# One fused kernel of two graph layers and two expert layers: the last expert layer's rows are placed in groups of chunks 0+1, 2 and 3 instead of 0, 1+2 and 3

## The reference

```
x = x + gnn0(layernorm(x), adj)              # filtered adjacency times features
x = x + ffn0(layernorm(x))                   # 8 experts, top 2, all rows through all experts
x = x + gnn1(layernorm(x), adj)              # normalised adjacency times features, ELU
def ffn1(x):                                 # x here is layernorm(x)
    h = rmsnorm(x, ln1)
    q, k, v = rope(h wq), rope(h wk), h wv                # 4 query heads, 2 key heads of 32
    y = softmax(q k / sqrt(32), causal) v                 # 2048 x 2048 scores
    x = x + y wo
    f = rmsnorm(x, ln2)
    p = softmax(f router_w); tp, ti = top_k(p, 2); tp = tp / (sum(tp) + 1e-9)
    return x + sum over the 2 chosen experts of tp * (silu(f w1) * (f w3)) w2
x = x + ffn1(layernorm(x))
```

## Time and profile before

| what | us |
| --- | --- |
| three runs: lowest, median, highest | 610.11, 612.19, 612.92 |
| the profiled execution, its span | 610.4 |
| PE, DVE, ACT, POOL busy in it | 501.5, 429.3, 314.3, 254.2 |
| attention chunk 2 (12 steps) | about 377.7 to 424.5 |
| attention chunk 3 (16 steps) | about 424.5 to 489.4 |
| chain of chunk 3, first experts' blocks, late row scatters | 489.4 to 531 |
| the other blocks and the way out | 531 to 610.4 |

### The profile page before, as it was taken

The page is one execution under the profiler, slowest core; times in us unless marked ns, Lnnn a source line. Parts: engine busy times, 40 slices in busy tenths (PEclk is TensorE's granted clock), DMA queues, the critical chain, the costliest instruction groups (busy, mean ns, idle before and its releaser), DMA issues.

```text
span 610.4 us, 11302 instructions
## 1 busy us (share of the span) xinstructions
PE 501.5 (82%) x3819; PEld 281.4 (46%) x3819; DVE 429.3 (70%) x1065; ACT 314.3 (51%) x522; POOL 254.2 (42%) x275
## 2 busy tenths in 40 slices
PE   2999986699999799996776888998969657498880
PEld 1533334477777445443322432333412157397770
DVE  6898838888999925757786896999752038166564
ACT  0787985869999001201254453764745334166661
POOL 3000005133436401102364895997353632555562
PEclk9999995999999799999578789999989859599996
DMA  8999954100139250110233522003035447389925
GB/s 302 409 421 422 405 189 149 42 19 20 34 129 411 85 109 0 39 26 15 68 110 99 157 72 60 2 1 104 35 129 177 176 121 222 112 277 384 324 89 175
DMA packets 39570, 93.43 MB, mean 153 GB/s; under 512 B 7488, under 2 KB 24944, under 8 KB 35168
## 3 DMA queue, kind: packets, MB, share of 16 engines
q1 hardware_dynamic: 35072, 86.96, 40.6%
q0 software_dynamic: 2272, 4.69, 2.2%
q10 hardware_dynamic: 2176, 1.13, 0.6%
HBM read 69.39 MB, written 21.00 MB: 148 GB/s over the span
## 4 chain that ended last, share of the span: by engine, by line
PE 54%; DVE 21%; ACT 7%; issue 6%; another core or an unknown queue 5%; DMA 4%; POOL 1%; SPq 1%; DVEq 0%; POOLq 0%; ACTq 0%
PE ps L1578 8%; DVE A L2385 7%; PE ps L1755 6%; PE ps L1489 6%; PE ps L1506 6%; PE ps L1404 5%; PE ps L1859 3%; PE ps L1656 3%; PE ps L1747 3%; DMA R<-in_adj_in 3%; PE ps L1842 2%; PE ps L1603 2%; PE ps L1381 1%; DVE bst L1916 1%
## 5 line engine op out<-in xcount | busy, mean ns | idle before, releaser
L2385 DVE TENSOR_REDUCE A<-ps 128x1 f32<-128x512 f32 (+3 forms) x160 | 86.3, 601 | 13.7 <-PE ps L1656 13.0
L1302 ACT ACTIVATE A<-ps 128x1024 f32<-128x1024 f32 (+3 forms) x80 | 68.4, 894 | 49.2 <-PE ps L1747 40.3
L1007 POOL TENSOR_TENSOR G<-G,A 128x1024 f32<-128x1024 f32 (+3 forms) x40 | 73.8, 1888 | 9.1 <-ACT A L1302 8.9
L1656 PE MATMUL ps<-A 96*128 96x512 f16 (+3 forms) x160 | 55.4, 388 | 10.4 <-DVE A L2385 5.1
L1578 PE MATMUL ps<-A,G 128*128 128x512 f32 x128 | 62.1, 611 | 0.0
L1404 PE MATMUL ps<-R,G 128*128 128x512 f32 x128 | 59.2, 605 | 1.0 <-DVE G L1959 0.8
L1859 PE MATMUL ps<-A 128*128 128x128 f16 (+1 forms) x702 | 50.3, 228 | 6.0 <-issue 6.0
L1506 PE MATMUL ps<-R 128*128 128x128 f16 x768 | 48.2, 219 | 6.7 <-DVE x L2077 5.8
L1506 PEld LDWEIGHTS ps<-R 128*128 128x128 f16 x768 | 45.3, 98 | 14.3 <-issue 6.6
L1747 PE MATMUL ps<-A 97*128 97x512 f16 (+3 forms) x160 | 45.2, 366 | 6.9 <-ACT A L1302 5.1
L2059 DVE SCALAR_TENSOR_TENSOR R<-R 128x512 f16<-128x512 f32 x64 | 46.7, 754 | 5.0 <-ACT R L1157 4.7
(11 more groups left out here) (311 smaller groups left out, 933.0 us busy)
## 6 DMA issues: line engine op xcount, KB each, us to landing
A<-w_split SPq DMA_DIRECT2D x39, 533.0 KB
A<-in_adj_t SPq DMA_DIRECT2D x16, 1024.0 KB, 17.5
slots_in<-xn SPq DMA_DIRECT2D x1, 8320.0 KB, 22.4
R<-in_adj_in SPq DMA_DIRECT2D x7, 1024.0 KB, 6.1
w_split<-A SPq DMA_DIRECT2D x9, 725.0 KB, 4.1
xn<-in_adj_in SPq DMA_DIRECT2D x5, 1024.0 KB
xT<-in_adj_in SPq DMA_DIRECT2D x4, 1024.0 KB
A<-in_f_w SPq DMA_DIRECT2D x16, 170.5 KB
```

The source lines that it names most:

```text
L1007: pool.tensor_tensor(total, total, probabilities(n, pair)[:, :, t0:CW], ALU.add).then_inc(s_sum, 1)
L1302: act.activation(probabilities(n, pair)[:, :, t0:CW], ps[:, 2 * pair:2 * pair + 2, t0:CW], ACT.Exp, scale=1.0 / (SQ * SQ * float(HD) ** 0. ...
L1656: last = pe.matmul(ps[:, bank, 0:width], queries(t // TPC, h)[0:KQ, P * (t % TPC):P * (t % TPC) + P], keys(b, h // (NH // NKV))[0:KQ, 0:wi ...
L2385: dve.reduce_max(pm[:, h, t % TPC, b:b + 1], ps[:, bank, 0:width], AX_X).then_inc(s_rmf, 1)
```

## The change

The groups become 8, 4 and 4 tiles (`GTS`), so group 0 holds chunks 0 and 1, group 1 chunk 2, group 2 chunk 3. Chunk 1's units `out`, `stats`, `rows` and `tr` move from chunk 3's steps into chunk 2's, its `router_root` on POOL too; `dt` and `db` of chunk 1 come two steps earlier. `choose`, `exp`, `weigh` and `rank` of group 0 move to steps 1 and 2 of chunk 3, `rows`, `tr` and `rows2` of chunk 2 to steps 3 and 4. All 24 row scatters in chunk 3's steps now wait for exponentials, one for each, from the ninth of chunk 3 on: 16 of group 0, then 8 of group 1. The pass over the last expert's weights on POOL (`low_weights(7)`) stands after the first 8. The spare columns in which group 0 and group 1 keep their tables are exchanged, since group 0 is now the wide one. Neither the number of scatters nor what is computed changes.

```diff
-GTS = (TPC, 2 * TPC, TPC)
+GTS = (2 * TPC, TPC, TPC)
...
-                v.append(free_cols(1 + g, o, n))
+                v.append(free_cols((2, 1, 3)[g], o, n))
...
-                       (2, 7): [("dt", 1)], (2, 8): [("db", 1)], (2, 11): [("choose", 0)],
-                       (3, 0): [("dt", 2), ("out", 1), ("db", 2), ("exp", 0)],
-                       (3, 1): [("out", 2), ("stats", 1), ("stats", 2), ("weigh", 0)],
-                       (3, 2): [("rows", 1), ("rows", 2), ("rank", 0)], (3, 4): [("tr", 1), ("tr", 2)],
-                       (3, 5): [("logit", 1), ("logit", 2), ("choose", 1), ("rows2", 1), ("rows2", 2)],
+                       (2, 5): [("dt", 1)], (2, 6): [("db", 1)], (2, 7): [("out", 1), ("stats", 1)],
+                       (2, 9): [("rows", 1)], (2, 10): [("tr", 1)],
+                       (3, 0): [("dt", 2), ("logit", 1), ("db", 2), ("rows2", 1)],
+                       (3, 1): [("out", 2), ("choose", 0), ("stats", 2)],
+                       (3, 2): [("exp", 0), ("weigh", 0), ("rank", 0)], (3, 3): [("rows", 2)],
+                       (3, 4): [("tr", 2), ("rows2", 2)], (3, 5): [("logit", 2), ("choose", 1)],
                        (3, 6): [("exp", 1), ("weigh", 1)], (3, 7): [("rank", 1)]}
...
-        PACE = 2 * (len(steps) - len([c for c, _ in steps if c == NC - 1]) + 11)
+        LAST_CHUNK_AT = 2 * len([c for c, _ in steps if c < NC - 1])
+        ROWS_FROM = (LAST_CHUNK_AT + 8, LAST_CHUNK_AT + 8 + 2 * GTS[0])
...
+                if (c, turn) == (2, 8):
+                    router_root(1)
...
-            router_root(1)
             router_root(2)
-            pool.wait_ge(s_fn, NC - 1)
+            pool.wait_ge(s_fn, 2)
...
-                        if g == 1:
-                            pool.wait_ge(s_p, min(2 * len(steps), PACE + (4 * (2 * t + which)) // 5))
+                        pool.wait_ge(s_p, min(2 * len(steps), ROWS_FROM[g] + 2 * t + which))
                         scatter_rows(g, t, which)
-
-            pool.wait_ge(s_fn2, 1)
+                    if (g, t) == (0, TPC - 1):
+                        low_weights(7)
+
+            pool.wait_ge(s_fn2, 2)
             scatter_group(0)
-            low_weights(7)
+            pool.wait_ge(s_fn, NC - 1)
             pool.wait_ge(s_fn2, NC - 1)
             scatter_group(1)
```

## The result

| | before | changed |
| --- | --- | --- |
| median of 4 runs on the same chip, us | 611.75 (610.11 to 612.92) | 616.42 (614.89 to 617.96) |
| ratio, with its 95% interval | | 1.0107 (1.0063 to 1.0151) |
| span of the profiled execution | 610.4 | 613.1 |

The changed kernel is slower by 1.1%; forecast were 608.7 us and a gain of 3.5. In this document medians are of all runs, and ratios leave out those in which the chip was in a slower state (3 of the 10 of `spread`, 1 of the 10 of `spread_root_inside`, and some of the kernel before).

What follows compares the result with a forecast made beforehand. Chunk 2 was taken as bound by DVE, chunk 3 as losing 16.0 us of PE time to POOL's row scatters. +2.6 + 0.4 - 6.5 = -3.5 us gave a median of 608.7 us, range 600.5 to 617.0.

Steps and rivals of the forecast that it cites:

- Chunk 2, DVE: Chunk 2: work added on DVE, which has only 0.9 us to spare, lengthens the chunk by 2.6 us.
- The check whether DVE comes to `rows` ahead of the root: End of chunk 2: POOL's root done by 417, DVE at `rows` about 418.5, so no cost unless POOL slips.
- Early chunk 3: First steps of chunk 3 on PE: +2.1 us of waiting less 1.7 of work moved away, net +0.4.
- The wait for `rank`: Early chunk 3: PE waits 2.1 us ahead of `rank` until DVE's `choose` for 8 tiles ends.
- The scatters: Chunk 3: 19 paying row scatters at 0.5 us leave 9.5 of 16.0 us lost, a gain of 6.5.
- The size of the loss before: Chunk 3's second part in the kernel before: 16.0 us of PE time lost while POOL runs row scatters.
- The spacing of 1.41 us: Chunk 3: waiting for exponentials, two in 2.83 us, puts one scatter every 1.41 us instead of 1.28.
- rival 1: Chunk 3: the spacing is enough and PE loses nothing to scatters; -13.0 us, 599.2; chance 0.17.
- The beat: Exponentials in steps 6 to 15 of chunk 3: 3.6 to 3.8 us a step would show the forecast.
- Rival 3: Chunks 2 and 3: +3.0 us is paid and scatters in one long run cost 1.0 each; +6.0, 618.2; chance 0.14.
- Forecast span 606.9: Whole kernel, profiled execution: 610.4 less 3.5 us; the runs' median was forecast at 608.7.

Runs made afterwards that it cites:

- spread: Changed kernel with chunk 1's row scaling on ACT, rank one step later, root one earlier, scatters at wider spacing and nine after the last exponential: 609.19 us, ratio 0.9985.
- spread_root_inside: The kernel of spread with the last chunk's root ahead of the last three of the 24 row scatters: 612.79 us, ratio 1.0053.
- no_pace: Changed kernel without any pacing, its 24 row scatters going as soon as positions are there: 624.91 us, ratio 1.0261.
- rows_by_twos: Changed kernel with DVE's row scaling going through every second element, even ones first, then odd: 615.28 us, ratio 1.0090.
- twelve_at_half_pace: Changed kernel with 12 row scatters at every second exponential, the other 12 after the last: steps 4 to 15 of chunk 3 took 37.48 us.

## Why the prediction was wrong

**Chunk 2, DVE (+2.6, measured +9.70).** This is the step that failed. It counted `rows` as 0.87 us, from a row in which POOL did nothing, and moved it beside POOL's additions, where it took 5.10; and it put nothing down for the clock behind PE's wait. The same prediction took 2.85 us off a `choose` row because a pass on POOL had held it, and did not ask where else that would happen. With the scaling off DVE and the root in time the addition is 2.52 us; the rest, 7.2, is 4.23 of DVE standing, and what PE lost at the lower clock: at a mean of 0.67 over 9.8 us some 3.2 (an estimate; the two make 7.4). In six other executions of the same order chunk 2 grew by 8.98 to 9.17. The check whether DVE comes to `rows` ahead of the root came out as said (root ready at 413.81, DVE there at 415.66). It was the wrong thing to be afraid of.

**Early chunk 3 (+0.4, measured +3.37).** The wait for `rank` was right to 0.1 us (2.02 for 2.1). But the 0.6 us of `tr` that PE saves lie behind this stretch, and chunk 1's logit product, 0.45, came into it. Above all the wait was costed at its length: at a mean clock of 0.66 over the 5 us from 441 on, PE lost 1.7 more. 2.0 + 1.7 + 0.45 - 1.1 for `out` is 3.1. Without the 1.7 it is 1.4, and the executions whose clock stayed at 1.00 had 1.72. Whether the clock falls behind this wait is thus chance as far as the runs show. Moving the wait away gave 2.15 of the attention.

**The scatters (-6.5, measured -9.27).** The size of the loss before was right: 16.0 worked out, 16.8 measured. The price was not: 9.5 us should have stayed and 7.6 did. It was taken as one figure for each paying scatter, from pairs in the tail; the runs show that it depends on how closely and how long they follow each other, from nothing to 0.86 us. The spacing of 1.41 us, on which the forecast and rival 1 rest, did not come about. The prediction had the first scatter some 5 us earlier than before, and POOL unable to pile up work; it started 15.7 us after chunk 3's first exponential (15.3 before), since it waits for DVE, and POOL then made up for its lateness in runs 1.29 us apart. (The wait lets the first scatter go when eight exponentials of chunk 3 are done, not nine, which changed nothing.) The beat was hit (3.77 for 3.6 to 3.8) as a mean only, the stops stayed stops. That 7.6 lies near 9.5 is therefore partly luck. The size of the loss before, 16.0, also held slower products, which the prediction did not separate.

**Rivals.** Rival 3 had the sign and nearly the place (DVE's longer chunk 2 and the wait for `rank` are paid), but laid its price on the scatters. None of the rivals had the row scaling. Forecast span 606.9, plus 7.1, plus 3.0, minus 2.8 for these three, plus 1.84 - 2.25 - 0.74 for the stretches that the change does not touch, gives 613.1, the span that was measured. Of the 4.7 us between the medians the three terms explain 9.70 + 3.37 - 9.27 = 3.8.

**Left open.** Why short rows of 8 bytes cost PE more (48.30, one execution) than full ones (45.12). How a POOL instruction holds PE at all, and whether it is PE that stands. The prediction said so because DVE starts on a router product only at 448.50 that should end at 443.95. But by the same trace PE began products behind it in the meantime:

```profile
446.79 1.28 PE L1755 MATMUL ps<-A,ones 128*32 128x512 f32 x8
```

Either these rows are earlier than PE's real work, or the signal that the product is ready came late. No run tells the two apart; "PE stands" above means that its results come late.

## What to carry to other kernels

Before an operation is moved to another time, ask for each of its instructions what runs on the other engines at the new place, and take its duration from a row with the same neighbour; a duration from an idle neighbour is a lower bound. A wait put on PE costs more than its length when the clock falls behind it, and it need not fall each time. An experiment that moves one thing to the end may take others with it, so look at every engine and at the DMA share before the difference is put down to that thing. Row scatters from POOL should be spread out, here to one in 2.8 us; but what waits for the last of them sets how far they may be spread, so the gain of 16 us in one stretch was worth nothing until the reader of the rows could also wait.

## What the runs showed of the hardware

- PE's results come late while POOL issues indirect transfers closely: 24 at starts 1.29 us apart with one pause cost 20.7 us, 12 at mostly 2.8 us cost 0.0, 24 in runs of up to 7 cost 7.6, and 24 of 16 rows of 8 bytes still cost 44.96 - 37.48 = 7.5. Loads at over 400 GB/s beside the attention cost nothing in twelve_at_half_pace.
- Four row scalings on DVE, state buffer to state buffer, took 5.10 us beside POOL's additions and 0.87 without; the statistics and maxima beside the same additions took no longer than usual. Each scaling ended 0.08 to 0.09 us behind the end of one operation of POOL.
- After 5.17 us without work PE's granted clock was 0.67 in the next 9.8 us. After 2.02 us it was 0.66 in the 5 us from 441 on, and after the same wait in three other executions (2.01 us in no_pace and rows_by_twos) it stayed at 1.00.
